# Odd rows moved to partitions 64 and up in a convolution chain, with projection, w3 and attention sums as pairs of column-half matmuls

## The reference

```
L0: q,k,v = batchnorm(x) @ w_qkv; q,k centred, squared, normalised
    kv = k2^T v (per image, 48x48); attn = (v + q2 kv/64) @ w_ln + b
    y  = leaky(concat(attn, x) @ w1 + b1)            # 96 channels
    y  = leaky(conv3x3(y, w2) + b2); x = y @ w3 + b3 + x
L1: relu -> depthwise 3x3 -> pointwise 48x48 -> batchnorm
L2: rw = sigmoid(mean(x) @ Wr + br)                  # 4 experts mixed per image
    h = relu(bn(x @ Wk(rw)))  (48->192); h = relu(bn(depthwise3x3(h, rw)))
    x = bn(h @ Wk2(rw)) + x   (192->48)
L3: as L1
```

## Time and profile before

| | |
|---|---|
| median of 3 runs | 1258.3 us (1257.62 to 1258.52) |
| the profiled execution's own time | 1259.41 us |
| its span, first to last instruction | 1257.6 us |
| TensorE busy | 1168.3 us (93%) |
| VectorE busy | 849.4 us (68%) |
| ScalarE busy | 473.0 us (38%) |
| mean granted TensorE clock | 0.969 of 2.4 GHz |
| one full iteration | 141.48 us |

### The profile page before, as it was taken

One profiled execution on the slowest core, in us unless ns is written; L12 is line 12 of the kernel. 1 busy time (PEld: TensorE's weight loads), 2 busy tenths in 40 slices (PEclk: granted clock), 3 DMA queues, 4 the chain that ended last, 5 costly groups with the idle time before them and its releaser, 6 DMA issues.

```text
span 1257.6 us, 14703 instructions
## 1 busy us (share of the span) xinstructions
PE 1168.3 (93%) x4981; PEld 754.2 (60%) x4981; DVE 849.4 (68%) x1154; ACT 473.0 (38%) x812; POOL 90.4 (7%) x72
## 2 busy tenths in 40 slices
PE   4799879999999999999999999999999999998976
PEld 3556566656665676656665676656665676655434
DVE  4541369975599369975599369975599369972950
ACT  3211324335522544335522544335522544333421
POOL 0200002000200002000200002000200002000000
PEclk9699869999999999999999999999999999999997
DMA  4031623069403873069403873069303870069125
GB/s 58 15 47 21 75 46 38 1 88 133 59 5 44 112 89 38 0 87 133 58 5 44 112 89 38 0 87 133 58 4 44 112 89 1 1 88 134 26 36 74
DMA packets 213132, 72.91 MB, mean 58 GB/s; under 512 B 206349, under 2 KB 206962, under 8 KB 213106
## 3 DMA queue, kind: packets, MB, share of 16 engines
q1 hardware_dynamic: 213106, 72.58, 45.6%
HBM read 10.51 MB, written 6.29 MB: 13 GB/s over the span
## 4 chain that ended last, share of the span: by engine, by line
PE 81%; DVE 6%; ACT 4%; issue 4%; DMA 2%; SPq 2%; POOL 0%; ACTq 0%; DVEq 0%; POOLq 0%
PE bank L1065 32%; PE bank L1089 9%; PE bank L1018 4%; PE bank L1076 4%; PE bank L1047 4%; DVE dwa L629 3%; PE bank L1007 3%; PE bank L1155 3%; PE bank L1156 3%; PE bank L1092 3%; PE bank L1091 3%; PE bank L1104 3%; PE bank L1133 2%; PE bank L1105 2%; PE bank L1039 2%
## 5 line engine op out<-in xcount | busy, mean ns | idle before, releaser
L1065 PE MATMUL bank<-y_parts,w_h 96*96 96x512 f32 x1152 | 301.3, 410 | 0.0
L629 DVE SCALAR_TENSOR_TENSOR dwa<-h1a,dyn,dwa 128x1024 f32<-128x1024 f32 x240 | 293.5, 1273 | 0.0
L1065 PEld LDWEIGHTS bank<-y_parts,w_h 96*96 96x96 f32 x1152 | 186.5, 162 | 98.0 <-issue 14.1
L629 DVE SCALAR_TENSOR_TENSOR dwb<-h1b,dyn,dwb 128x1024 f32<-128x1024 f32 x128 | 154.8, 1274 | 0.0
L1065 PE MATMUL bank<-y_parts,w_l 96*96 96x512 f32 x576 | 147.8, 401 | 0.0
L1089 PE MATMUL bank<-a_parts,wt_h 128*96 128x512 f32 x384 | 120.9, 424 | 23.3 <-DMA y_parts<-a_parts 14.8
L1065 PEld LDWEIGHTS bank<-y_parts,w_l 96*96 96x96 f32 x576 | 93.4, 162 | 44.3
L1089 PEld LDWEIGHTS bank<-a_parts,wt_h 128*96 128x96 f32 x384 | 60.8, 166 | 54.5 <-issue 20.0
L943 POOL TENSOR_TENSOR y_parts<-y,y_parts 96x512 fp32r<-96x512 f32 x56 | 67.1, 1199 | 210.1 <-DVE y L668 210.1
L1315 ACT ACTIVATE y<-bank,b2s 96x512 f32<-96x512 f32 x32 | 21.9, 683 | 157.9 <-PE bank L1065 157.9
L707 DVE SCALAR_TENSOR_TENSOR a_parts<-v,a_parts 96x512 fp32r<-96x512 f32 x64 | 43.3, 685 | 50.8 <-ACT a_parts L1343 48.0
(11 more groups left out here) (223 smaller groups left out, 1683.3 us busy)
## 6 DMA issues: line engine op xcount, KB each, us to landing
y_parts<-a_parts SPq DMA_DIRECT2D x32, 396.0 KB, 6.1
y_parts<-a_parts SPq DMA_DIRECT2D x64, 192.0 KB, 6.6
tok<-in_x_dram SPq DMA_DIRECT2D x48, 192.0 KB, 4.8
a_parts<-a_parts SPq DMA_DIRECT2D x32, 264.0 KB, 3.3
x_even<-y_parts SPq DMA_DIRECT2D x16, 384.0 KB, 9.0
x_odd<-y_parts SPq DMA_DIRECT2D x16, 384.0 KB, 7.8
out_dram<-dwb SPq DMA_DIRECT2D x32, 192.0 KB, 3.6
y_parts<-a_parts SPq DMA_DIRECT2D x32, 132.0 KB, 4.3
```

Source lines behind the costliest of these rows:

```text
L629: nc.vector.scalar_tensor_tensor(out=dst, in0=tap_input(n, t), scalar=weight, in1=dst, op0=ALU.mult, op1=ALU.add).then_inc(tap_step, 1)
L1065: last = nc.tensor.matmul(bank[0:C2, :], wgt[:, t, :], src[:, rows, cols], start=t + n == 0, stop=t == TAPS - 1 and n == 2)
```

## The change

Odd rows move from partitions 48 to 95 to partitions 64 to 111 (`ODD_AT = 64`, `P2 = 112`) in every tile of the pair layout. The even and odd results of projection's `pc` products, of w3 and of the attention sums are now computed by two matmuls of 48 (w3: 64) columns each, one into partitions 0 up, one into 64 up of the same bank; their weights hold no zero half. In the sums k becomes the stationary operand and x the moving one (97 columns), and a new small matmul (`attention_gather`) adds and transposes the two halves. The own rows leave partitions 48 to 63 and 112 to 127 free for the shifted copies, so `copy_beside` has 8 DMAs where it had 7 (one of 32 partitions becomes two of 16). L1, L3, pick and the transposes have 112 columns for 96. More tiles are cleared during setup.

The order changes too: TensorE transposes the next image's x behind L1 chunks 0 and 1, computes all its scores there, and only then takes projection chunks 2 and 3 and L1 chunks 2 and 3; L3 chunk 0 comes ahead of routing; the sums come ahead of L3 chunk 3; the halo ahead of the attention weights. ScalarE follows that order, with `finish_unit` 4 and 5 between the score groups; VectorE runs `norms_begin` ahead of L1's last two low parts.

```diff
@@ TensorE
-                for par in range(2):
-                    cols = slice(C - C * par, 3 * C - C * par)
-                    nc.tensor.matmul(bank[0:C2, :], pick[:, cols], ...)
-                    nc.tensor.matmul(bank[0:C2, :], pc[:, 0, cols], first[:, :, par, :], ...)
-                    last = nc.tensor.matmul(bank[0:C2, :], pc[:, 1 + m // 2, cols], other[:, :, par, :], ...)
+                for par in range(2):
+                    to = slice(ODD_AT * (1 - par), ODD_AT * (1 - par) + P2)
+                    nc.tensor.matmul(bank[0:P2, :], pick[:, to], x2[par][...], start=par == 0, stop=False)
+                for n, (part, src) in enumerate(((0, first), (1 + m // 2, other))):
+                    for par in range(2):
+                        last = nc.tensor.matmul(bank[par * ODD_AT:par * ODD_AT + C, :], pc[:, part, :], src[:, :, par, :],
+                                                start=False, stop=n == 1)
@@ w3
-                    last = nc.tensor.matmul(bank[0:C2, :], w3eo[:, par, :], rows[:, :, par, :], start=par == 0, stop=par == 1)
+                    last = nc.tensor.matmul(bank[par * ODD_AT:(par + 1) * ODD_AT, :], w3p[:, :], rows[:, :, par, :], start=True, stop=True)
@@ attention_sums
-                for par in range(2):
-                    for i in range(RUN):
-                        last = nc.tensor.matmul(bank[0:SUMS, 0:C], token(par, i, X_AT, SUMS), token(par, i, K_AT, C), ...)
+                for i in range(RUN):
+                    for par, at in enumerate((0, ODD_AT)):
+                        last = nc.tensor.matmul(bank[at:at + C, 0:SUMS], token(par, i, K_AT, C), token(par, i, X_AT, SUMS), ...)
+            def attention_gather(image):
+                pe.wait_ge(gs_ready, 2 * image + 2)
+                nc.tensor.matmul(ring_a.bank(A_G)[0:SUMS, 128:128 + C], gs[:, :], twin[:, :], start=True, stop=True).then_inc(gt_done, 1)
@@ VectorE, sums_out
+                for at in (0, ODD_AT):
+                    nc.vector.tensor_copy(gs[at:at + C, :], bank[at:at + C, 0:SUMS]).then_inc(gs_ready, 1)
@@ SP, copy_beside
-            for to, frm in ((own[C2:128, :, behind, :], own[0:BEHIND, :, below, :]),
-                            (dst[0:rest, :, here, :], own[BEHIND:C, :, below, :]),
-                            (dst[rest:APART, :, here, :], own[C:C2, :, above, :])):
+            for to, frm in ((own[C:ODD_AT, :, behind, :], own[0:SPARE, :, below, :]),
+                            (own[P2:128, :, behind, :], own[SPARE:2 * SPARE, :, below, :]),
+                            (dst[0:rest, :, here, :], own[2 * SPARE:C, :, below, :]),
+                            (dst[rest:APART, :, here, :], own[ODD_AT:P2, :, above, :])):
@@ TensorE, iteration
-                l1(f, (0, 1))
-                project(back, (2, 3)); transpose_x(attn, (0, 1)); l1(f, (2,)); transpose_x(attn, (2, 3)); l1(f, (3,))
-                attention_scores(attn); routing(f); l3_and_out(back)
-                attention_sums(attn); out_tokens(back, (3,)); attention_weights(attn); expand_halo(f)
+                for m in range(2):
+                    l1(f, (m,)); transpose_x(attn, (2 * m, 2 * m + 1))
+                attention_scores(attn); project(back, (2, 3)); l1(f, (2, 3)); l3(back, (0,)); routing(f)
+                l3(back, (1,)); out_tokens(back, (0,)); l3(back, (2,)); out_tokens(back, (1,)); attention_sums(attn)
+                l3(back, (3,)); out_tokens(back, (2,)); attention_gather(attn); out_tokens(back, (3,))
+                expand_halo(f); attention_weights(attn)
```

More of the change, by code:

```diff
@@ L843, in copy_beside @@
             for part in range(2):
-                for to, frm in ((dst[APART:APART + rest, part, here, 1:W + 1], own[BEHIND:C, part, below, 0:W]),
-                                (dst[APART + rest:128, part, here, 1:W + 1], own[C:C2, part, above, 0:W])):
+                for to, frm in ((dst[APART:APART + rest, part, here, 1:W + 1], own[2 * SPARE:C, part, below, 0:W]),
+                                (dst[APART + rest:128, part, here, 1:W + 1], own[ODD_AT:P2, part, above, 0:W])):
                     sp.dma_start(to, frm).then_inc(b_copied[n][half], 16)
@@ L1213, in iteration @@
                 if back is not None:
+                    l3(back, (3,))
+                    out_tokens(back, (2,))
+                if attn is not None:
+                    attention_gather(attn)
+                if back is not None:
                     out_tokens(back, (PCHUNKS - 1,))
+                expand_halo(f)
                 if attn is not None:
                     attention_weights(attn)
-                expand_halo(f)
                 conv1(attn, f)
@@ L1246, in x_out, with scores_out @@
                     act.wait_ge(xt_done, 4 * image + n + 1)
-                    nc.scalar.activation(xcm[0:C2, n * BANK:(n + 1) * BANK], ring_a.bank(A_XT + n)[0:C2, :], ACT.Copy)\
+                    nc.scalar.activation(xcm[0:P2, n * BANK:(n + 1) * BANK], ring_a.bank(A_XT + n)[0:P2, :], ACT.Copy)\
                         .then_inc(xcm_ready, 1)
-            def scores_out(image):
-                for n in range(8):
+            def scores_out(image, groups):
+                for n in groups:
                     act.wait_ge(qk_done, 8 * image + n + 1)
@@ L1396, in iteration @@
                     project_affine(back, f + 1, 1)
-                l1_out(f, (0,))
+                for m in range(2):
+                    l1_out(f, (m,))
+                    if attn is not None:
+                        x_out(attn, (2 * m, 2 * m + 1))
+                if attn is not None:
+                    scores_out(attn, range(0, 3))
                 if back is not None:
                     finish_unit(back, 4)
+                if attn is not None:
+                    scores_out(attn, range(3, 6))
+                if back is not None:
                     finish_unit(back, 5)
-                l1_out(f, (1,))
+                if attn is not None:
+                    scores_out(attn, range(6, 8))
                 if back is not None:
@@ L1421, in iteration @@
                 if back is not None:
-                    l3_and_tokens_out(back, (2, 3))
+                    l3_out(back, (0,))
+                route(f)
+                if back is not None:
+                    l3_and_tokens_out(back, (1, 2, 3))
                     tokens_out(back, (PCHUNKS - 1,))
```

285 lines of the change are left out of this document (148 added, 137 removed).

## The result

Before 1258.41 us (median of 4), after 1308.57 us (1303.95 to 1309.57, 4 runs): ratio 1.0391, 95% interval 1.0365 to 1.0417. The change makes the kernel 3.9% slower. The prediction said 1226 us, range 1202 to 1252, with a chance of 0.85 for faster: the sign is wrong and the range misses. The profiled execution took 1303.95 us, its span 1302.1.

A forecast was written before the change was run, and what follows sets the result against it. TensorE (1168.3 of 1257.6 us busy), with VectorE also full before layer 1, bounds the kernel. Six iterations at 2.4 us give 14.4; with 4.3, 5 and 9, less 1 for setup, 31.7 off 1258.3: 1226 us, range 1202 to 1252.

The forecast's parts named there:

- rival C: Paired matmuls of 512 columns take turns instead of running at once; 1266 us, chance 0.12.
- A change of shape: On TensorE, switching between a pair and differently shaped neighbours was charged 0.07 us each, bounds nothing and 0.14.
- The Trainium skill's drain at a mode switch: TensorE drains when tiling mode changes: 0.43 us a change, 16 an iteration, total near 1240; held to 0.14 at most.
- The three waits that were named: TensorE waits 3.8 us at layer 1's chunk 0, 1.4 at the scores, 3.5 at layer 3's chunk 0.
- The fourth: TensorE waits 0.9 us at layer 3's chunk 2 for the second half's copies.
- The dependence of the second half on layer 1's chunk 3: Layer 3's second copy batch starts only after layer 1's chunk 3, 92.3 us after VectorE's first tap, landing about 104.
- the halo at S+115.6 ... the period is 136.5, against 141.48: 5.0 us less: Halo 115.6 us after VectorE's first tap (S), plus 20.85 to the next; 5.0 us of 11.6 saved is kept.
- The clock: TensorE at 1.2 GHz around the two longer waits costs 2.6 us an iteration, bounds 0 and 6.
- The copies: Layer 3's copy batch takes 10.7 us: 10.3 from issue to quiet, plus 0.4 for one more DMA.
- the margin: Before the change, copies land 2.6 us before TensorE wants them at layer 1's chunk 0.
- Rival E: Waits and clock cost more: batches 1 us longer, two low stretches behind each wait; 1240 to 1257 us, chance 0.11.
- Ahead of and behind the loop: Outside six full iterations: image 0's sums gain 4.3, image 1's 5, iteration 7 and the end 9; setup costs 1 us.

The follow-up runs named there:

- the kernel with filler and table mended: Changed kernel with the router's activation ahead of `root_of_q` and idle matmuls in both waits for copies: 1267.5 us.
- the table mended: Changed kernel with the router's activation put back ahead of `root_of_q` on ScalarE: 1281.9 us.
- experiment 3: Changed kernel with 16 idle matmuls ahead of layer 1's chunk 0 and 18 ahead of layer 3's chunk 0: 1275.5 us.
- 1267.1: Kernel with scores directly ahead of layer 3 and ScalarE's order mended, but scores moved back ahead of projection 2 and router behind layer 3's chunk 0: 1267.1 us.
- 1220.1: Changed kernel with projection 2 and 3 first, scores directly ahead of layer 3, router ahead of layer 3 and ScalarE's order largely put back: 1220.1 us.
- experiment 5: Series on the changed kernel moving projection 2 and 3, the scores, the router and ScalarE's steps around layer 3's copies: 1220.1 to 1306.7 us.
- experiment 6: Series on pairs and layout with the old order (1220.8 us) and on the 1220.1 us kernel: transposes moved, idle matmuls, one depthwise tap moved; 1203.9 to 1221.9 us.

## Why the prediction was wrong

**Right.** The pairs run at once at full size: 2.3, 1.0 and 2.88 us against 2.3, 1.0 and 2.7 to 2.8 forecast, and rival C is out. A change of shape takes about 0.09 us where I charged 0.07: from pick to the first pair 0.33 us pass (698.12 to 698.45), from one pick to the other 0.24. The Trainium skill's drain at a mode switch (TensorEngine Tiling (Array Packing), Key Properties) does not show beyond that: pick, pairs and w3 stand without a gap in the rows above. (My own sum for that rival was off: 6 us less 2.5 is 3.5 an iteration and 21 in six, which makes 1247 and not 1240.) The three waits that were named are where they were put: 4.3 us (forecast 3.8) at layer 1's chunk 0, 1.2 (1.4) at the scores, 4.9 (3.5) at layer 3's chunk 0. The fourth, 0.9 at layer 3's chunk 2, came only where the clock was mended (1.2 to 1.7 us in the kernels with idle matmuls). The dependence of the second half on layer 1's chunk 3 was seen too.

**The step that failed** is the sum "the halo at S+115.6 ... the period is 136.5, against 141.48: 5.0 us less", with 2.6 for the clock. Measured, in the iteration shown: halo at S+124.3, period 148.5, so 12.0 in place of 2.6 above 136.5. Its terms, from the same milestones:

- *The clock*, 2.6 charged, about 5.6 measured. I had taken one stretch as long as that of iteration 0, and some of a second. There are three: S+63 and S+100, twice as long, and one at S+128 of which I had no thought. The forecast has 8.8 us from layer 1's chunk 0 to the end of the wait-free work ahead of the scores, the trace 11.4 (2.6 more); 1.8 more lie behind layer 3's chunk 0 (the kernel with filler and table mended takes 21.4 us from there to the halo, after 23.2). Behind the halo it is 1.2: 24.2 us to the next S, against 21.7 with the table mended, less the load's 1.28. The filler (experiment 3) bears the first two out: it has the halo of this iteration 3.8 us earlier, where the two come to 4.4.
- *The copies*, 10.7 a batch, measured 12.4 and 12.5 in this iteration, at two places: 1.3 us at layer 1's chunk 0 and 1.8 at layer 3's. Most of this was a wrong reading of the kernel before. I had taken "quiet" for "landed": the DMA engines are quiet from 688.6, but the last of the seven DMAs, issued at 683.4, tells of its landing 6.7 us later, at 690.1:

```profile
L846 SPq DMA_DIRECT2D y_parts<-a_parts x1: 1073/1073/1073, 683.4 to 683.4; - x1
...
DMA to landing us min/median/max: 6.7/6.7/6.7
```

  So that batch took 11.8 us and not 10.3, and the margin, "what decides this change", was about 1.1 us and not 2.6. The eighth DMA, charged with 0.4, comes on top: SP issues for 7.8 us (695.70 to 703.53) where the earlier trace rows have 6.2. Like for like, at layer 3's chunk 0 of the two kernels in the new order, seven DMAs take 11.6 us from the first issue to the reader's start (735.54 to 747.10 with the order alone) and eight 12.5 (732.30 to 744.79).
- *The table load*, 1.28 us, not charged. `root_of_q` ahead of `route` stood in the diff, and the load's row was in ScalarE's timeline; I followed ScalarE's order only for its waits.
- *Layer 3 to the halo*, 1.3 us short in my sum even at full clock (20.1 forecast, 21.4 above).
- *The weights behind the halo*, 0.85 us, not charged: I took 20.85 us from halo to S over from before, and with the table mended it is 21.7.

These make 5.6 + 3.1 + 1.3 + 1.3 + 0.85 = 12.15.

**The question not asked.** The prediction priced each wait of the new order but never the old order with the pairs. That was 136.7 a period, and 1220.8 us in all. In other words its forecast of 136.5 gave the changed order for free what the pairs alone bring. It said that before "the scores and two L1 chunks covered this batch", and went on. Rival E named the right mechanisms with a chance of 0.11, and priced them at 1240 to 1257.

**Ahead of and behind the loop.** Up to the first S 8.3 us were forecast as a gain (5, 4.3, less 1), 10.7 came. For iteration 7 and the end 9 were forecast, and 3.8 were lost: there, too, the clock falls three times, at S+63, S+76 and S+97, where before it fell once.

**The whole loss** of about 88 us between after (1308.6) and the old order with pairs (1220.8), by runs: the table load and its stretch 26.7; moving the scores back from the kernel with the table mended (1281.9) 61.8, of which 47.0 go with the scores' place (1267.1 against 1220.1); the router moved in the same run, and its share was not parted, but the waits listed in experiment 5 leave it little. The other 14.8 lie between the runs at 1281.9 and 1267.1. These have the same order on TensorE and differ on ScalarE (`finish_unit`, x out, the scores' evacuations, `fourth_powers`, `root_of_q`) and in the place of `norms_begin` on VectorE; which of them counts was not parted. How a separate destination for layer 3's copies would do, which would free the second half from layer 1's chunk 3, was not tried.

## What to carry to other kernels

When work moves, price what it covered in its old place before what it does in the new one: here moving 6.9 us of scores laid open waits of 5 us for copies of 12 us, and brought the clock down with them. Price a reordering against the same change without it, not against the kernel before. And where an order on ScalarE changes, list which function each ACTIVATE uses: a table load of 1.3 us that slides onto the path cost 4 us an iteration, because the wait also took the clock down.

## What was not expected of the hardware

- Two column halves ran at once though they were issued two and two: in the kernel with the halves in runs the first passes of the two halves start 13 ns apart, 667.977 and 667.990 us. With 16 and 16 they did not, 5.25 us against 2.88. How far TensorE looks ahead between the two is not known from these runs.
- The clock's fall does not follow the longest wait alone. A filled wait of 4.5 us moved the fall to a later gap that had not dropped the clock before (experiment 6); periods then stood at 136.5; less the 1.6 us of such a stretch they would be 134.9.
- Eight DMAs of the wider layout take 12.5 us from the first issue to the reader's start where seven take 11.6, for the same bytes. And DMA engines that have gone quiet do not mean landed data: 1.5 us lay between the two in the kernel before (688.6 and 690.1 us).
